# Transformer block with attention and experts on one core: who takes the last head's peaks out of their banks

## The chip, the cores and the metric

The kernel runs on one core of a Trainium2 chip. A core has five engines that run at the same time, each through its own list of instructions, and wait for each other by semaphores: TensorE (matmul), VectorE, ScalarE, GpSimd and SyncE, which starts DMAs. The metric is the time of one execution in microseconds (us), as the median of several runs. Before the change it was 1334.45 us (three runs, 1333.49 to 1334.74).

## The reference, cut to what matters

```python
h = layernorm(x) * (1 + ca) + sa                   # x: 2048 tokens of 128
q, k, v = h @ wq.T, h @ wk.T, h @ wv.T             # 1024 columns each
q, k, v = (a.reshape(1, 16, 2048, 64) for a in (q, k, v))   # 16 heads of 2048 positions of 64
attn = softmax(q @ k^T * 64 ** -0.5) @ v           # for each head: 2048 x 2048 scores
x = x + ga * (attn.reshape(1, 2048, 1024) @ wo.T)
h = layernorm(x) * (1 + cb) + sb
s = sigmoid(h @ gate_w.T); sel = top_k(s + expert_bias, 2)   # 8 experts, 2 for each token
x = x + gb * (shared_expert(h) + sum over the 2 chosen e of
              s_e * w2[e] @ (silu(w1[e] @ (s_e * h)) * (w3[e] @ (s_e * h))))
```

The reshape makes head i out of the tokens 128 i to 128 i + 127: each of them gives 16 of the head's positions. Everything is computed in float32, the scores as three products of a high and a low part.

## The kernel before, in words

**Units.** A head is worked through as two units of half the queries (1024) each, so there are 32 units; the last head is units 30 and 31. A unit goes over 16 tiles of 128 keys. For each tile TensorE makes the scores of 128 keys and 1024 queries in two banks (lines 1230 to 1236, and 1242 for the first two tiles), ScalarE takes their exponential into one of eight buffers `probs` (line 818), TensorE multiplies it by V (line 1254, "a weighing"), and GpSimd adds the tiles up for the softmax's denominator (lines 889 to 903). The scores of tile kt wait for exponential kt - 2.

**Peaks.** Before the exponentials of a unit the kernel needs a shift for each query, from the peak of its scores. These are found a unit ahead, from 16 "pairs" per unit: TensorE multiplies 128 queries by two times 512 keys into banks 6 and 7 (line 1177), and something takes the maximum out of them. There is one such pair of banks in the units, so each pair waits on the semaphore `peak_free` until the pair before is out. Pairs 0 and all even ones, and 15, are taken by VectorE itself, by a maximum straight from the banks (`pair`, line 975). Pairs 1, 3, ..., 13 (`TAKEN`) are first copied by ScalarE into the buffer `peak_copy` (`take_pair`, line 760), which frees the banks, and VectorE takes the maximum of the copy later (`taken`, line 985), which frees `peak_copy` for the next copy (`copy_read`). After pair 15 the maxima go to TensorE to be turned (line 1185), and by DMA to where the next unit's first scores read them.

**The plan.** `side_jobs` writes the order out by hand: a unit has 32 places, four for each two tiles of keys: scores, scores, weighing, weighing. Jobs are put behind a place, and every engine goes through the same list and does its part of each job. Pairs 4 to 15 of the next unit are behind places 1, 3, ..., 23 of a unit, pairs 0 to 3 of the one after that behind places 25 to 31. The maximum of a copied pair ("taken") is two places behind its pair. In unit 30 there are only pairs 4 to 15 (for unit 31), in unit 31 there are none.

**Other jobs of unit 30.** The softmax sum of unit 29 (place 6, line 1267), its inverse in four parts on VectorE (`inv`, places 6, 7, 8 and 10, line 1001), the scaling of the outputs (place 11, line 1008), the output projection (place 22, line 1280). New in the last head is the norm before the experts, for the first 12 blocks of 128 tokens: statistics of four blocks at a time on VectorE behind the pairs at places 5, 9 and 13 (lines 340 and 349), the root on ScalarE behind place 15 (line 368, with a table load for Sqrt and one back to Exp), the reciprocal on VectorE behind place 17 (lines 356, 518, 519), and the norm itself on ScalarE, four blocks each behind places 18, 22 and 26 (line 498).

**Unit 31 and after.** The logits (line 1204, place 4), the gate on VectorE, a chain of ten instructions of which each waits for the one before, but for the pair of comparisons (lines 527 to 543), the token weights turned (line 1209, place 19) and spread by DMA. Then 36 experts' items of 512 tokens: two matmuls (lines 464 and 465), Silu on ScalarE (506), products on VectorE (571, 573), output product (450) for the item before. The tokens of a routed item are weighed ahead of it by line 438: the first three on VectorE, the others on GpSimd, behind its last add (line 889).

Of the kernel before, what the change touches and what calls it, by code (L numbers as in the profile page):

```python
# [35 lines left out]
EARLY_PAIRS = 4  # L36

TAKEN = list(range(1, PEAK_PAIRS - 1, 2))
# [42 lines left out]
def side_jobs(half, sums=True, project=True, pairs=True, early=True, last_head=False):  # L81

    places = [[] for _ in range(4 * PAIRS)]
    for place, (kind, i) in LONG_JOBS[half].items():
        if sums if kind in ("sum", "out") else pairs if kind == "shift" else project:
            places[place].append((kind, i))
    if pairs:
        for i in range(EARLY_PAIRS, PEAK_PAIRS):
            places[2 * (i - EARLY_PAIRS) + 1].append(("pair", i))
    if early:  # L90
        for i in range(EARLY_PAIRS):
            places[2 * (PEAK_PAIRS - EARLY_PAIRS + i) + 1].append(("pair", i))

    for i in TAKEN:
        place = 2 * ((i - EARLY_PAIRS) % PEAK_PAIRS) + 1
        if pairs if i >= EARLY_PAIRS else early:
            places[min(place + 2, 4 * PAIRS - 1)].append(("taken", i))
    if project:
        for place, job in LOW_PLACES[half].items():
            places[place].append(job)  # L100
    if sums:
        for place, job in SCALE_PLACES[half].items():
            places[place].append(job)
    if last_head:
        for place, jobs in LAST_HEAD_PLACES[half].items():
            places[place] += jobs
    return [places[4 * step:4 * step + 4] for step in range(PAIRS)]


def build(nc, x, wq, wk, wv, wo, gate_w, w1, w2, w3, sw1, sw2, sw3, expert_bias, cond, wmod, out):  # L110
    with ExitStack() as ctx:
# [141 lines left out]
        def adds(kt):  # L253


            return kt // 2 + 1 if kt < 4 else kt - 1
# [6 lines left out]
        def units(t):  # L263

            first, last = (isinstance(t, int) and t == 0), (isinstance(t, int) and t == HEADS // 2 - 1)
            for p in (0, 1):
                for half in (0, 1):
                    final_head = last and p == 1
                    plan = side_jobs(half, sums=not (first and p == 0 and half == 0), project=not final_head,
                                     pairs=not (final_head and half == 1), early=not final_head,  # L270
                                     last_head=final_head)
                    yield p, half, t * 2 + p, t * 4 + (2 * p + half), plan
# [15 lines left out]
        END_T = HEADS // 2 - 1  # L288
# [406 lines left out]
        def _(act):  # L695
# [104 lines left out]
            def body(t):  # L800
                local = 0
                for p, half, head, unit, plan in units(t):
                    first = isinstance(t, int) and t == 0 and p == 0 and half == 0
                    last_head = isinstance(t, int) and t == END_T and p == 1
                    if half == 0 and not last_head:
                        copy_head(head + 1)
                    for step, places in enumerate(plan):
                        for place, jobs in enumerate(places):
                            if place < 2:
                                kt = 2 * step + place  # L810
                                act.wait_ge(scored, unit * TILES + (kt + 1))
                                if not (first and kt < PROBS):

                                    old = kt - PROBS
                                    if kt % 2 == 0:
                                        act.wait_ge(pv_done, unit * PAIRS + (old // 2 + 1))
                                    act.wait_ge(added, unit * ADDS + (adds(old % TILES) - (ADDS if old < 0 else 0)))
                                act.activation(probs[:, kt % PROBS, :],  # L818
                                               ps[:, 2 * place:2 * place + 2, :].rearrange("p a b -> p (a b)"),
                                               ACT.Exp, scale=SCALE).then_inc(exped, 1)  # L820

                            for kind, i in sorted(jobs, key=lambda job: job[0] != "pair"):
                                if kind in COUNTED:
                                    side(Job(jobs_at(t) + local), kind, i, 1 - p)
                                if kind == "step k":
                                    round_step(Job(jobs_at(t) + (local - 1)), i, 1 - p, head * 2 + (3 + i))
                                if kind == "pair" and i in TAKEN:
                                    target = unit + (1 if i >= EARLY_PAIRS else 2)
                                    take_pair(i, target * PEAK_PAIRS + i, target)
                                if kind == "sum":  # L830
                                    sums.append(jobs_at(t) + local + 1)
                                if kind in ("turn", "logits", "weights"):
                                    gating_act(act, kind, i)
                                if kind == "root":
                                    layernorm_root(act, range(READY_BLOCKS), 5)
                                if kind == "norm":
                                    norm_act(act, range(4 * i, 4 * i + 4), 2)
                                local += kind in COUNTED
                        if step == 0 and not first:
                            copy_pv(unit, sums[-1] if sums else None)  # L840
# [76 lines left out]
        def _(dve):  # L917
# [121 lines left out]
            def body(t):  # L1039
                local = 0  # L1040
                for p, half, head, unit, plan in units(t):
                    for places in plan:
                        for jobs in places:
                            for kind, i in jobs:
                                job = Job(jobs_at(t) + local)
                                if kind == "pair" and i not in TAKEN:
                                    target = unit + (1 if i >= EARLY_PAIRS else 2)
                                    pair(i, target * PEAK_PAIRS + i, target, PEAK_BANK)
                                if kind == "taken":
                                    target = unit + (1 if i >= EARLY_PAIRS else 2)  # L1050
                                    taken(i, target * PEAK_PAIRS + i, copies(target, i))
                                if kind == "low q":
                                    low_q(Job(jobs_at(t) + (local - 1)), i, 1 - p,
                                          head * CASTS + (CASTS + PROJECTIONS.index(("q", i)) + 1))
                                if kind == "step k":
                                    step_k(Job(jobs_at(t) + (local - 1)), i, head * 2 + (3 + i))
                                if kind == "low k":
                                    low_k(Job(jobs_at(t) + (local - 1)), i, 1 - p, head * 2 + (3 + i))
                                if kind == "inv":
                                    invert(i, Job(jobs_at(t) + (local - 1)))  # L1060
                                if kind == "scale":
                                    scale_outputs(Job(jobs_at(t) + (local - 1)), unit, 1 - half)
                                if kind == "out":
                                    add_head(head - 1, job)
                                if kind == "shift":
                                    keep_shift(job, unit + 1, 1 - half)
                                if kind == "stats":
                                    dve.wait_ge(mid_ready, 4 * i + 4)
                                    layernorm_stats(dve, link, x_mid, range(4 * i, 4 * i + 4))
                                if kind == "rstd":  # L1070
                                    shifts_of(dve, link, range(READY_BLOCKS), 3)
                                if kind == "gate":
                                    dve.wait_ge(consts, 5 + EXPERTS - 1)
                                    gate(dve, link, 0)
                                local += kind in COUNTED
# [305 lines left out]
```

## Time and profile before

| | |
|---|---|
| median of three runs | 1334.45 us |
| time of the profiled execution | 1334.12 us |
| its span, first to last instruction | 1332.3 us |
| TensorE busy | 1307.2 us (98%) |
| VectorE busy | 899.1 us (67%), 1024 instructions |
| ScalarE busy | 864.7 us (65%), 1052 instructions |
| GpSimd busy | 1175.7 us (88%) |
| copies `peak_copy` on ScalarE (line 760) | 215, mean 1016 ns |
| maxima from the banks on VectorE (line 975) | 297, mean 1223 ns |
| maxima from the copy on VectorE (line 985) | 215, mean 1212 ns |

Times in the rows are microseconds from the start of the span. PE is TensorE, PEld its weight loads, DVE VectorE, ACT ScalarE, POOL GpSimd. A busy share is an average over stages; what a stage waits for is read from its own rows. Matmuls overlap: a row of two that lasts 0.50 us may be followed by the next after 0.34.

### The profile page before, as it was taken

Reading aid. Unit: us, or ns where it says so; the run is one execution under the profiler, and the core shown is the slowest. Engines: PE = TensorE matmul, PEld = TensorE weight load, DVE = VectorE, ACT = ScalarE, POOL = GpSimd, SP = SyncE. Lnnn points to the kernel's source line nnn. Section 1 sums busy time; section 2 is a strip of 40 time slices with the busy share of each in tenths; the row PEclk is TensorE's granted clock in tenths of the full one; section 3 lists DMA queues with packets and bytes.
Section 4 is the critical chain, followed back from the end, with each engine's and each line's share of the span. In section 5 each row is a group of like instructions: output and inputs, shape, how many; then the busy total and the mean of one; then the engine's idle time right before and its main releaser. Section 6 shows DMA issues by size and latency. Waiting matters only on the chain.

```text
span 1332.3 us, 21996 instructions
## 1 busy us (share of the span) xinstructions
PE 1307.2 (98%) x8714; PEld 692.3 (52%) x8714; DVE 899.1 (67%) x1024; ACT 864.7 (65%) x1052; POOL 1175.7 (88%) x537
## 2 busy tenths in 40 slices
PE   6999999999999999999999999999999999999998
PEld 5554555454555545454545555554545455454565
DVE  5767667676767676676767676766767676736754
ACT  6676767666766666676767666666767676675331
POOL 2399999999999999999999999999999999989343
PEclk8999999999999999999999999999999999999999
DMA  8020202020100102020201002020202011003222
GB/s 208 3 47 1 49 1 49 1 48 1 36 14 5 45 1 49 1 49 1 48 1 28 21 1 48 2 48 1 49 1 48 1 25 25 1 1 64 71 96 56
DMA packets 31960, 41.53 MB, mean 31 GB/s; under 512 B 4298, under 2 KB 15186, under 8 KB 31858
## 3 DMA queue, kind: packets, MB, share of 16 engines
q1 hardware_dynamic: 31714, 40.13, 12.4%
q8 instruction: 69, 1.13, 0.4%
q14 instruction: 33, 0.27, 0.1%
q10 hardware_dynamic: 144, 0.00, 0.0%
HBM read 13.70 MB, written 1.11 MB: 11 GB/s over the span
## 4 chain that ended last, share of the span: by engine, by line
PE 94%; DVE 3%; ACT 1%; issue 1%; DMA 0%; SPq 0%; ACTq 0%; DVEq 0%
PE ps L1254 35%; PE ps L1177 13%; PE ps L1230 9%; PE ps L1236 9%; PE ps L1233 9%; PE ps L1154 4%; PE ps L1280 2%; PE ps L1158 2%; PE ps L464 2%; PE ps L450 2%; PE ps L1267 2%; PE ps L465 2%; DVE peak_parts L975 1%; PE ps L1242 1%; DMA probs<-in_L_attn_wq_dram 0%
## 5 line engine op out<-in xcount | busy, mean ns | idle before, releaser
L818 ACT ACTIVATE probs<-ps 128x1024 f32<-128x1024 f32 x512 | 498.8, 1033 | 76.8 <-PE ps L1236 72.7
L975 DVE TENSOR_REDUCE peak_parts<-ps 128x2 f32<-128x1024 f32 x297 | 362.2, 1223 | 243.9 <-PE ps L1177 242.3
L1254 PE MATMUL ps<-probs,v_sb 128*64 128x512 f32 x2048 | 522.6, 606 | 0.0
L903 POOL TENSOR_TENSOR acc<-acc,probs 128x1024 f32<-128x1024 f32 x192 | 458.2, 2387 | 31.8 <-ACT probs L818 30.2
L903 POOL TENSOR_TENSOR acc_odd<-acc_odd,probs 128x1024 f32<-128x1024 f32 x192 | 459.7, 2394 | 0.0
L760 ACT COPY peak_copy<-ps 128x1024 f32<-128x1024 f32 x215 | 218.4, 1016 | 247.7 <-PE ps L1177 169.9
L985 DVE TENSOR_REDUCE peak_parts<-peak_copy 128x2 f32<-128x1024 f32 x215 | 260.6, 1212 | 34.1 <-ACT peak_copy L760 34.1
L1254 PEld LDWEIGHTS ps<-probs,v_sb 128*64 128x64 f32 x2048 | 123.8, 136 | 156.6 <-issue 116.0
L1230 PE MATMUL ps<-q_hi,d_hi 64*128 64x512 f32 x512 | 201.6, 394 | 1.2 <-ACT probs L818 1.2
L1230 PE MATMUL ps<-q_hi,d_swap_hi 64*128 64x512 f32 x512 | 201.6, 394 | 0.0
L1236 PE MATMUL ps<-q_hi,d_lo 64*128 64x512 f32 x512 | 200.4, 391 | 0.0
L1236 PE MATMUL ps<-q_hi,d_swap_lo 64*128 64x512 f32 x512 | 200.4, 391 | 0.0
L1233 PE MATMUL ps<-q_lo,d_hi 64*128 64x512 f32 x512 | 199.7, 390 | 0.0
L1233 PE MATMUL ps<-q_lo,d_swap_hi 64*128 64x512 f32 x512 | 199.4, 389 | 0.0
L1177 PE MATMUL ps<-k_hi,q_hi 64*128 64x512 f32 x512 | 120.3, 466 | 4.4 <-DVE d_lo L966 2.3
L1177 PE MATMUL ps<-k_swap_hi,q_hi 64*128 64x512 f32 x512 | 117.8, 456 | 3.5 <-ACT peak_copy L760 1.8
L1177 PEld LDWEIGHTS ps<-k_hi,q_hi 64*128 64x128 f32 x512 | 47.8, 183 | 130.6 <-DVE peak_parts L975 68.1
L1177 PEld LDWEIGHTS ps<-k_swap_hi,q_hi 64*128 64x128 f32 x512 | 48.0, 184 | 127.6 <-DVE peak_parts L975 54.9
L1001 DVE RECIPROCAL ps<-ps 128x128 f32<-128x128 f32 x128 | 112.9, 928 | 0.0
L1233 PEld LDWEIGHTS ps<-q_lo,d_hi 64*128 64x128 f32 x512 | 94.7, 185 | 12.7
L1230 PEld LDWEIGHTS ps<-q_hi,d_swap_hi 64*128 64x128 f32 x512 | 95.0, 186 | 10.5 <-ACT probs L818 0.4
L1236 PEld LDWEIGHTS ps<-q_hi,d_lo 64*128 64x128 f32 x512 | 94.5, 185 | 11.4
(159 smaller groups left out, 1496.9 us busy)
## 6 DMA issues: line engine op xcount, KB each, us to landing
k_swap_hi<-k_hi SPq DMA_DIRECT2D x64, 128.0 KB, 2.3
d_swap_hi<-d_hi SPq DMA_DIRECT2D x64, 128.0 KB, 2.3
d_swap_lo<-d_lo SPq DMA_DIRECT2D x64, 128.0 KB, 2.4
q_hi<-weights_dram SPq DMA_DIRECT2D x8, 256.0 KB, 3.1
q_lo<-weights_dram SPq DMA_DIRECT2D x8, 256.0 KB, 3.2
k_hi<-weights_dram SPq DMA_DIRECT2D x8, 256.0 KB, 3.2
k_swap_hi<-weights_dram SPq DMA_DIRECT2D x8, 256.0 KB, 3.2
probs<-in_L_ffn_w_dram SPq DMA_DIRECT2D x2, 512.0 KB, 5.6
```

The source lines that it names most:

```text
L760: act.copy(peak_copy[:, :, :], ps[:, PEAK_BANK:PEAK_BANK + 2, :]).then_inc(peak_free, 1)
L818: act.activation(probs[:, kt % PROBS, :], ps[:, 2 * place:2 * place + 2, :].rearrange("p a b -> p (a b)"), ACT.Exp, scale=SCALE).then_inc( ...
L903: pool.tensor_tensor(total, total, probs[:, kt % PROBS, :], ALU.add).then_inc(added, 1)
L975: dve.tensor_reduce(peak_parts[:, :, i // STRETCHES, i % STRETCHES], ps[:, bank:bank + 2, :], AX.X, ALU.max).then_inc(peak_free, 1)
L985: dve.tensor_reduce(peak_parts[:, :, i // STRETCHES, i % STRETCHES], peak_copy[:, :, :], AX.X, ALU.max).then_inc(copy_read, 1)
L1001: dve.reciprocal(job.ps[:, cols], job.ps[:, cols]).then_inc(part_inverted, 1)
L1154: mm = pe.matmul(job.ps[at:at + HEAD_DIM, k * P:(k + 1) * P], w[:, col:col + HEAD_DIM], h_head[:, :], start=True, stop=True, tile_position ...
L1177: mm = pe.matmul(ps[:, bank + b, :], q_hi[at, target_parity, q:q + P], keys[at, target_parity, cols], start=True, stop=True, tile_position ...
L1230: pe.matmul(ps[:, slot + b, :], hi[b][at[b], p, cols], q_hi[at[b], p, q], start=kt < 2, stop=False, tile_position=(b * HEAD_DIM, 0), skip_ ...
L1233: pe.matmul(ps[:, slot + b, :], hi[b][at[b], p, cols], q_lo[at[b], p, q], start=False, stop=False, tile_position=(b * HEAD_DIM, 0), skip_g ...
L1236: mm = pe.matmul(ps[:, slot + b, :], lo[b][at[b], p, cols], q_hi[at[b], p, q], start=False, stop=kt >= 2, tile_position=(b * HEAD_DIM, 0), ...
L1254: mm = pe.matmul(ps[at:at + HEAD_DIM, PV_BANK, :], v_sb[:, p, chunk_of(kt) * HEAD_DIM:(chunk_of(kt) + 1) * HEAD_DIM], probs[:, kt % PROBS, ...
```

## The change

In the last head, and only there, no pair is copied. `side_jobs` plans no "taken" job there, ScalarE skips its copies, and VectorE takes the maximum of the odd pairs straight from the banks, at the pair's own place.

```diff
@@ side_jobs
     for i in TAKEN:
         place = 2 * ((i - EARLY_PAIRS) % PEAK_PAIRS) + 1
-        if pairs if i >= EARLY_PAIRS else early:
+        if (pairs if i >= EARLY_PAIRS else early) and not last_head:
             places[min(place + 2, 4 * PAIRS - 1)].append(("taken", i))
@@ ScalarE's body
-                                if kind == "pair" and i in TAKEN:
+                                if kind == "pair" and i in TAKEN and not last_head:
                                     target = unit + (1 if i >= EARLY_PAIRS else 2)
                                     take_pair(i, target * PEAK_PAIRS + i, target)
@@ VectorE's body
                 for p, half, head, unit, plan in units(t):
+
+                    last_head = isinstance(t, int) and t == END_T and p == 1
                     for places in plan:
                         for jobs in places:
                             for kind, i in jobs:
                                 job = Job(jobs_at(t) + local)
-                                if kind == "pair" and i not in TAKEN:
+                                if kind == "pair" and (last_head or i not in TAKEN):
                                     target = unit + (1 if i >= EARLY_PAIRS else 2)
                                     pair(i, target * PEAK_PAIRS + i, target, PEAK_BANK)
```

## Rows read from the trace of the kernel before

**Rows 1.** Busy time by stretches: stretch, its length, each engine's busy time (instructions), clock, DMA.

```profile
1156.60:1180.00 23.40, 19.42 (x134) 9.79 (x134) 16.90 (x40) 17.33 (x23) 19.97 (x10) 1.00 0.00 1
1180.00:1195.00 15.00, 15.00 (x102) 8.85 (x98) 1.67 (x3) 9.35 (x13) 14.61 (x7) 1.00 0.01 1
```

**Rows 2.** Timeline, TensorE, unit 30: start, length, line, tiles, form, [idle before <-releaser]. P7, P10, P12 to P14.

```profile
1156.63 0.51 PE L1177 MATMUL ps<-k_swap_hi,q_hi 64*128 64x512 f32 x2
...
1163.09 0.49 PE L1177 MATMUL ps<-k_swap_hi,q_hi 64*128 64x512 f32 x2 [0.34 <-ACT peak_copy L760]
...
1168.11 0.50 PE L1177 MATMUL ps<-k_hi,q_hi 64*128 64x512 f32 x2 [0.34 <-ACT peak_copy L760]
...
1170.41 0.50 PE L1177 MATMUL ps<-k_hi,q_hi 64*128 64x512 f32 x2
...
1175.40 0.49 PE L1177 MATMUL ps<-k_swap_hi,q_hi 64*128 64x512 f32 x2 [1.45 <-ACT peak_copy L760]
```

**Rows 3.** Timeline, ScalarE, unit 30.

```profile
1168.07 1.28 ACT L368 ACT_TABLE_LOAD   x1
...
1170.99 1.94 ACT L818 ACTIVATE probs<-ps 128x1024 f32<-128x1024 f32 x2
...
1174.35 0.99 ACT L760 COPY peak_copy<-ps 128x1024 f32<-128x1024 f32 x1
```

**Rows 4.** Timeline, VectorE, unit 30.

```profile
1157.18 2.56 DVE L1001 RECIPROCAL ps<-ps 128x128 f32<-128x128 f32 x3
1159.65 1.16 DVE L975 TENSOR_REDUCE peak_parts<-ps 128x2 f32<-128x1024 f32 x1
...
1161.85 0.86 DVE L340 BATCH_NORM_STATS2 stats<-x_mid 128x6 f32<-128x128 f32 x4
...
1163.04 0.93 DVE L1001 RECIPROCAL ps<-ps 128x128 f32<-128x128 f32 x1
1164.00 0.69 DVE L1008 TENSOR_TENSOR oT<-o_raw,ps 128x512 f32<-128x512 f32 x1
1164.61 1.22 DVE L975 TENSOR_REDUCE peak_parts<-ps 128x2 f32<-128x1024 f32 x1
...
1175.94 1.23 DVE L975 TENSOR_REDUCE peak_parts<-ps 128x2 f32<-128x1024 f32 x1 [4.38 <-PE ps L1177]
```

**Rows 5.** Timeline, GpSimd, units 30 and 31, with its last add.

```profile
1181.78 2.37 POOL L903 TENSOR_TENSOR acc<-acc,probs 128x1024 f32<-128x1024 f32 x1 [0.32 <-ACT probs L818]
...
1198.10 3.07 POOL L897 TENSOR_TENSOR acc_odd<-probs 128x1024 f32<-128x1024 f32 x1 [2.19 <-ACT probs L818]
...
1231.48 2.34 POOL L889 TENSOR_TENSOR acc<-acc,acc_odd 128x1024 f32<-128x1024 f32 x1
```

**Rows 6.** Timeline, VectorE and TensorE, the first routed experts.

```profile
1231.62 2.75 DVE L573 TENSOR_TENSOR probs<-probs,q_hi 128x512 f32<-128x512 f32 x1
1231.83 1.02 PE L465 MATMUL ps<-acc,w3T 128*128 128x512 f32 x2
...
1236.10 1.13 PE L464 MATMUL ps<-acc,w1T 128*128 128x512 f32 x2 [0.51 <-DVE acc L438]
...
1240.88 1.02 PE L465 MATMUL ps<-acc,w3T 128*128 128x512 f32 x2
...
1242.63 1.02 PE L464 MATMUL ps<-acc,w1T 128*128 128x512 f32 x2
```

**Rows 7.** Timeline, ScalarE and VectorE, the first root of the prologue.

```profile
3.24 1.28 ACT L368 ACT_TABLE_LOAD   x1
...
4.04 0.18 DVE L349 BATCH_NORM_AGGREGATE mean_var<-stats 128x2 f32<-128x6 f32 x1
```

**Rows 8.** Timeline, VectorE, the gate in unit 31.

```profile
1195.54 0.44 DVE L527 TENSOR_SCALAR wvT<-wvT 128x96 f32<-128x96 f32 x1 [12.69 <-ACT wvT L486]
...
1197.97 0.95 DVE L535 TENSOR_TENSOR wkT<-wvT 128x768 f32<-128x768 f32 x1
...
1207.39 2.35 DVE L543 TENSOR_TENSOR wvT<-wvT 128x96 f32<-128x96 f32 x1
```

## The prediction

> **What bounds the kernel now.** The page's first part (the table above) has TensorE busy for 98% of the span, so the first question is where the last head is not TensorE. The table by stretches answers it [rows 1]: between 1156.6 and 1180.0 us, inside the last head's first unit, TensorE is busy for 19.42 of 23.40 us, and in the next 15 us for all 15.00. So 4.0 us of idle time are there to be had, and nothing in the next stage. I name a pair by its number i and write P10 for TensorE's two matmuls of pair 10; only one pair fits in the two peak banks, so each P waits until the pair before is out. The timeline of TensorE gives the starts [rows 2]: P10 waited 0.34 us and P14 1.45 us, both for ScalarE's copy. ScalarE's timeline shows why P14 is so late [rows 3]: Sqrt's table from 1168.07, the root, Exp's table, two exponentials from 1170.99, four norms (by the code), and only at 1174.35 the copy of pair 13, though P13 had started at 1170.41. VectorE's timeline [rows 4] is a full queue (three inversions, a pair, its copied neighbour, statistics, an inversion, the scaling); what is in front of a pair there is what will hold the bank after the change.
>
> The end hangs on GpSimd as well. Its adds [rows 5] run nearly without a break, with 0.32 us idle before 1181.78 and 2.19 before 1198.10, both for ScalarE's exponentials. Their last one ends at 1231.48 + 2.34 = 1233.82; VectorE's product at 1231.62 lasts 2.75 us, to 1234.37, just behind it, and the third routed expert's matmul starts at 1236.10 [rows 6]. A gain has to pass both engines.
>
> **What goes and what comes.** Units 30 and 31 are the last head, and pairs 4 to 15 of unit 31 are made in unit 30; the four early ones come from the unit before and are unchanged. So five copies (pairs 5, 7, 9, 11, 13; the last one took 0.99 us) go from ScalarE, and five reductions of the copy from VectorE. Five reductions from the banks, of 1.22 or 1.23 us, take their place, earlier in VectorE's order: pair 9 after inversion 3 and before the scaling, pair 11 after the third statistics, pair 13 after the reciprocal of the root. No DMA moves. VectorE's total hardly changes; which pair waits for what changes.
>
> Unit costs, from rows 2 and 4: a pair's start to its reduction 0.54 (1175.40 to 1175.94); reduction 1.22 or 1.23, the next instruction 0.08 before its end (1164.00 + 0.69 against 1164.61), so 1.14 apart; end of a reader to the next P 0.05 (1174.35 + 0.99 to 1175.40); from a P that waited, over two weighings, to the next 2.30 (1168.11 to 1170.41); an inversion 0.82 (a third of 1157.18 to 1159.65); statistics with moments 1.19 (1161.85 to 1163.04).
>
> P5 and P6 move by under 0.15 us, and the sum job behind them waits for GpSimd's last add anyway, so I let P7 stand at 1156.63. Then VectorE: pair 7 from 1157.17; inversions 1 and 2 from 1158.31; pair 8 at 1159.95; statistics at 1161.09; inversion 3 at 1162.28; pair 9 from 1163.10 to 1164.33. P10 is at 1164.38, not 1163.09: **1.29 us lost**, since statistics and an inversion that lay behind a copied pair now lie in front of a bank.
>
> P11 follows at 1166.68. The third statistics start at 1166.06 and end 1.27 later, at 1167.33; pair 11 runs from 1167.25 to 1168.48; P12 at 1168.53 (0.42 late), P13 at 1170.83, pair 13 from 1171.37 to 1172.60, **P14 at 1172.65 instead of 1175.40: 2.75 us gained**, because neither tables nor norms stand in front of the reader any more. On ScalarE the copy of pair 11 no longer precedes the Sqrt load. That load doesn't wait for its operand: in the prologue it starts at 3.24 while the moments end at 4.22 [rows 7]. So the root starts 0.05 after 1167.33 and exponential 8 another 1.62 later (from 1168.07 to 1170.99 are 2.92, less the first load and its gap of 0.02), at 1169.00 instead of 1170.99: 1.99 earlier, in time for P13's followers.
>
> The Trainium skill ("ScalarE: Activation LUTs", What ACT_TABLE_LOAD costs) adds a drain of about 1.38 us to a load of 1.28. The trace has no room for it [rows 3]: two loads, the root and all gaps lie within the 2.92 us from 1168.07 to 1170.99. By the page exponential 8 would be at about 1170.4, P14 at 1173.05, and the gain 2.35: it stands beside rival B.
>
> **What the later stages leave of it.** TensorE is full from 1180 to 1195 [rows 1], so it carries 2.75 on. GpSimd carries less: its backlog moves by the 1.99 of exponential 8 and eats the 0.32 of idle time, 2.34 in all (with 0.03 of overlap). The add before the idle time of 2.19 ended at 1198.10 - 2.19 = 1195.91, and would end at 1193.57. Now the gate [rows 8]. Its first step, at 1195.54, lasts 0.44 us, to the end of that add; it would be issued at 1192.79, and end at 1193.63, thus 2.35 earlier. The comparison of line 535 then comes at 1195.63, but GpSimd's next add, tied to exponentials that moved 2.75, at 1195.35. Before, the add came 0.13 us behind the comparison and lasted 3.07 against 2.37; now it comes in front. I take it that it has the first turn, as soon as line 534 is through (0.09 behind 535's issue, 1195.72), and ends 2.25 later, as 1198.10 + 3.07 = 1201.17 is 2.25 after line 535's end: at 1197.97. Line 535 and the next add then cost one round more, about the 3.07 that a hindered add took, to 1201.04. The rest of the gate, which took 8.57 from 1201.17 to 1207.39 + 2.35 = 1209.74, ends at 1209.61: only 0.13 earlier. TensorE's weight turns wait there, some 2.6 us, and nearly all its lead is gone at the start of the experts. GpSimd loses 0.25 net: three hindered adds as before, and 0.25 on the first (1195.35 to 1197.97 are 2.62, against 2.37). Its last add ends 2.50 earlier, at 1231.32. But there the time comes back: VectorE's product of 1231.62, now at 1231.49, finds GpSimd done and no longer waits for it. TensorE's own queue then sets the third routed expert [rows 6]. From the line 465 matmul before it, over one output product, to its line 464 matmul went 4.27 us (1231.83 to 1236.10); two experts later, unhindered, the same step took 1.75 (1240.88 to 1242.63). So it starts at 1231.83 + 1.75 - 0.13 = 1233.45 instead of 1236.10. **Gain 2.65.** If the comparison keeps its turn instead, gate and GpSimd both move 2.34, and the gain is 2.34. I take 2.6.
>
> That the two block each other for a whole instruction is what the skill states ("SBUF — State Buffer", Who interferes with whom), for two inputs in SBUF against GpSimd's reads, and never for a reduction. The trace agrees: 3.07 against 2.37 us. It says nothing of who is next in line, where my two sums part.
>
> The profiled execution took 1334.12 us around a span of 1332.3; less 2.6 it is 1331.5. The three runs have their median 0.33 higher, at 1334.45: forecast 1331.8.
>
> **Bounds.** The reduction of an odd pair behind VectorE's queue is in no row. Its price at P10 lies between 0 (pair 9 as soon as it is there) and 1.29 plus one statistics, 2.5; the gain at P14 doesn't rest on it if P11 to P13 keep to 2.30, and falls to about 1.5 at the far end. The gate's phase lies between 2.34 earlier and two GpSimd adds later than mine.
>
> **Rivals.** (A) The gate loses one turn more to GpSimd, for example because line 534 is caught too: it ends 2.3 later, at 1211.9, the experts start 2.2 late, the regain of 2.52 leaves 0.3: 1334.1. For it: line 543, on 128x96 elements, lasted 2.35 us, a whole add [rows 8]. Against: only line 535 changes its place by my sum. 10%. (B) Behind an exponential a table load takes twice its row: exponential 8 then starts 1.28 later than by my sum, at 1170.28, P13's followers wait for it and the next one, and P14 is at about 1173.0: 2.4 gained, 1332.1. For it: no load in rows 3 stands behind an exponential. Against: the second one, behind the root, took no more than 1.28 and a gap. 5%. (C) The other side: two turns more than mine, gate at 1214.2; the experts start 4.5 late and regain 2.52: 2.0 lost, 1336.5. It decides from a gate that ends after 1212.3. For it: every wait is a whole add of 2.3. Against: it takes an add 0.6 us earlier than I have it. 8%. (D) VectorE's queue costs more than I have and P14 gains only about 1.5: 1332.9. 12%.
>
> **Numbers.** The forecast has 65%; its own range, 2.2 to 3.2 us gained, is 1331.2 to 1332.3. What a measurement can tell from no change is about 0.2%, here 2.67 us, or 1331.8: the forecast sits on that line, so I give 42 of its 65 to faster and 23 to same, where A, B and D (27) fall too; C is slower. Faster 0.42, same 0.50, slower 0.08. The range goes to A's end and allows 0.3 us for the runs' spread: 1330.9 to 1334.2.
>
> **What would show it.** Right: P10 near 1164.4 after a wait of about 1.4 us for VectorE; ScalarE's Sqrt load right behind exponential 7, well before the root; P14 near 1172.6; the logits 2.7 earlier; line 535 some 3 us long; a wait of 2 to 3 us before the weight turns of line 1209; no long wait of VectorE at line 573. Wrong: P14 not before 1174, a load that waits for the moments, a gate that ends after 1210, or experts whose third product isn't over 2 us earlier.

## The result and the profile after

The changed kernel is slower: 1337.51 us (median of 17 runs, 1335.0 to 1338.34) against 1334.74 us for the kernel before (17 runs, 1333.49 to 1337.21), a ratio of 1.0015 with a 95% interval of [1.0008, 1.0021]. The forecast of 1331.8 us missed it, and so did its range, which ended at 1334.2. The profiled execution took 1337.32 us around a span of 1335.4, against 1334.12 around 1332.3. Lines from 1040 on have moved by two: the pairs are now at line 1179, the weighings at 1256, the output projection at 1282, the weight turns at 1211.

The changed kernel's page, engines and the three peak groups. The change did what it says: five copies fewer, five maxima more from the banks, five fewer from the copy. VectorE is busy for 3.8 us more, which no count explains.

```profile
PE 1310.5 (98%) x8714; PEld 694.9 (52%) x8714; DVE 902.9 (68%) x1024; ACT 860.3 (64%) x1047; POOL 1174.2 (88%) x537
...
L975 DVE TENSOR_REDUCE peak_parts<-ps 128x2 f32<-128x1024 f32 x302 | 368.2, 1222 | 239.6 <-PE ps L1179 237.9
...
L760 ACT COPY peak_copy<-ps 128x1024 f32<-128x1024 f32 x210 | 213.2, 1015 | 240.6 <-PE ps L1179 166.8
L985 DVE TENSOR_REDUCE peak_parts<-peak_copy 128x2 f32<-128x1024 f32 x210 | 254.5, 1212 | 34.1 <-ACT peak_copy L760 34.1
```

Its TensorE timeline in unit 30: P10, P12, P13, P14, the weighing and the output projection behind it, P15.

```profile
1164.44 0.50 PE L1179 MATMUL ps<-k_swap_hi,q_hi 64*128 64x512 f32 x2 [1.21 <-DVE peak_parts L975]
...
1168.56 0.50 PE L1179 MATMUL ps<-k_hi,q_hi 64*128 64x512 f32 x2
...
1170.86 0.51 PE L1179 MATMUL ps<-k_hi,q_hi 64*128 64x512 f32 x2
...
1176.03 0.50 PE L1179 MATMUL ps<-k_swap_hi,q_hi 64*128 64x512 f32 x2 [3.27 <-DVE peak_parts L975]
1176.46 1.55 PE L1256 MATMUL ps<-probs,v_sb 128*64 128x512 f32 x4
1177.79 3.16 PE L1282 MATMUL ps<-wo,oT 128*64 128x128 f32 x32
...
1181.75 0.50 PE L1179 MATMUL ps<-k_swap_hi,q_hi 64*128 64x512 f32 x2
```

P10 to P13 are where the forecast had them [rows 2]. P14 is not: it comes at 1176.03, 0.63 us later than before, where 2.75 earlier was forecast. VectorE's timeline of the same stretch shows what held pair 13:

```profile
1169.11 1.23 DVE L975 TENSOR_REDUCE peak_parts<-ps 128x2 f32<-128x1024 f32 x1 [0.60 <-PE ps L1179]
1170.25 0.22 DVE L356 RECIPROCAL rstd<-std 128x12 f32<-128x12 f32 x1
1170.50 2.06 DVE L518 TENSOR_TENSOR shift_ln<-mean_var,rstd 128x12 f32<-128x12 f32 x1
1172.59 2.26 DVE L519 TENSOR_SCALAR shift_ln<-shift_ln 128x12 f32<-128x12 f32 x1
1174.77 1.21 DVE L975 TENSOR_REDUCE peak_parts<-ps 128x2 f32<-128x1024 f32 x1
```

Two instructions on 128x12 elements take 4.3 us. Before, the same two took 0.17 us each, at 1171.17 and 1171.38, as VectorE's timeline of the kernel before has them:

```profile
1170.92 0.22 DVE L356 RECIPROCAL rstd<-std 128x12 f32<-128x12 f32 x1
1171.17 0.17 DVE L518 TENSOR_TENSOR shift_ln<-mean_var,rstd 128x12 f32<-128x12 f32 x1
1171.38 0.17 DVE L519 TENSOR_SCALAR shift_ln<-shift_ln 128x12 f32<-128x12 f32 x1
```

GpSimd's timeline of the changed kernel has the other side. Line 518 ends with the first of these adds (1170.15 + 2.38 = 1172.53), line 519 with the second (1172.48 + 2.34 = 1174.82):

```profile
1170.15 2.38 POOL L903 TENSOR_TENSOR acc<-acc,probs 128x1024 f32<-128x1024 f32 x1 [1.44 <-ACT probs L818]
1172.48 2.34 POOL L903 TENSOR_TENSOR acc_odd<-acc_odd,probs 128x1024 f32<-128x1024 f32 x1
```

and GpSimd's timeline of the kernel before shows why they didn't meet there: the add came when both were done, after a long idle time.

```profile
1172.09 2.38 POOL L903 TENSOR_TENSOR acc<-acc,probs 128x1024 f32<-128x1024 f32 x1 [3.35 <-ACT probs L818]
```

The add waits for exponential 8, and ScalarE's timeline of the changed kernel has that one at 1169.05, 1.94 earlier than before [rows 3]. The norms wait for line 519 too:

```profile
1164.53 1.28 ACT L368 ACT_TABLE_LOAD   x1
1167.43 0.30 ACT L368 ACTIVATE std<-mean_var,eps 128x12 f32<-128x12 f32 x1 [1.62 <-DVE mean_var L349]
...
1169.05 1.94 ACT L818 ACTIVATE probs<-ps 128x1024 f32<-128x1024 f32 x2
1174.89 1.65 ACT L498 ACTIVATE x_in<-x_mid,shift_ln,rstd 128x128 f32<-128x128 f32 x4 [3.90 <-DVE shift_ln L519]
```

The second loss is TensorE's clock. By the table of stretches the granted clock is still at 0.96 in the first stretch behind the wait of 3.27 us, which ended at 1176.03, and at 0.50 (1.2 of 2.4 GHz) in the three us after that:

```profile
1176.00:1177.00 1.00, 0.97 (x6) 0.44 (x8) 0.43 (x1) 1.00 (x3) 0.00 (x0) 0.96 0.00 0
1177.00:1180.00 3.00, 3.00 (x26) 2.39 (x24) 0.80 (x1) 2.89 (x6) 2.48 (x2) 0.50 0.03 5
1180.00:1181.00 1.00, 1.00 (x16) 0.93 (x14) 0.00 (x0) 0.00 (x0) 1.00 (x1) 0.83 0.00 0
```

The output projection takes 3.16 us instead of 1.92 and the weighing 1.55 instead of 1.08: 1.71 together. So P15 is 2.31 later (1181.75 against 1179.44), and the logits as much (1194.61 against 1192.31). Behind the logits the clock falls once more (0.50 from 1198 to 1200). The third routed expert is 2.61 later (1238.71, against 1236.10 in [rows 6]). TensorE waits for VectorE there, whose product of line 573 is again held by GpSimd's last add, and that add comes at 1234.08 instead of 1231.48. The three timelines, TensorE, VectorE and GpSimd:

```profile
1238.71 1.13 PE L464 MATMUL ps<-acc,w1T 128*128 128x512 f32 x2 [0.52 <-DVE acc L438]
...
1235.36 1.62 DVE L573 TENSOR_TENSOR probs<-probs,q_hi 128x512 f32<-128x512 f32 x1
...
1234.08 2.35 POOL L889 TENSOR_TENSOR acc<-acc,acc_odd 128x1024 f32<-128x1024 f32 x1
```

The rest of the 3.1 us of span is one meeting of VectorE and GpSimd more, of 0.47, near 1285, where a product of line 573 takes 1.81 us; a second profile of the kernel before has it too.

The gate never met the order that I feared, since the whole stage comes 2.3 later. VectorE's timeline of the changed kernel, gate:

```profile
1197.84 0.45 DVE L527 TENSOR_SCALAR wvT<-wvT 128x96 f32<-128x96 f32 x1 [12.67 <-ACT wvT L486]
...
1200.28 0.95 DVE L535 TENSOR_TENSOR wkT<-wvT 128x768 f32<-128x768 f32 x1
1201.27 0.96 DVE L537 TENSOR_TENSOR wkT<-wkT,earlier 128x768 f32<-128x768 f32 x1
1202.26 3.03 DVE L539 TENSOR_TENSOR wqT<-wqT,wkT 128x768 f32<-128x768 f32 x1
...
1207.62 2.34 DVE L543 TENSOR_TENSOR wvT<-wvT 128x96 f32<-128x96 f32 x1
```

### The profile page after: what moved, and what is told of

It reads as the page before. It is cut to its first block, busy times and chain, and to the rows that moved or that the text cites. A ratio compares the mean times of both kernels' runs of the same rounds, so it can differ in the third digit from the quotient of the medians.

```text
span 1335.4 us, 21986 instructions
## 1 busy us (share of the span) xinstructions
PE 1310.5 (98%) x8714; PEld 694.9 (52%) x8714; DVE 902.9 (68%) x1024; ACT 860.3 (64%) x1047; POOL 1174.2 (88%) x537
## 4 chain that ended last, share of the span: by engine, by line
PE 94%; DVE 4%; ACT 1%; DMA 0%; issue 0%; SPq 0%; DVEq 0%; ACTq 0%
PE ps L1256 36%; PE ps L1179 13%; PE ps L1232 9%; PE ps L1238 9%; PE ps L1235 9%; PE ps L1156 4%; PE ps L1282 2%; PE ps L1160 2%; PE ps L1269 2%; PE ps L464 2%; PE ps L450 2%; PE ps L465 2%; DVE peak_parts L975 1%; PE ps L1244 1%; DVE ps L1001 0%; DVE probs L573 0%
## 5 line engine op out<-in xcount | busy, mean ns | idle before, releaser
L975 DVE TENSOR_REDUCE peak_parts<-ps 128x2 f32<-128x1024 f32 x302 | 368.2, 1222 | 239.6 <-PE ps L1179 237.9
L760 ACT COPY peak_copy<-ps 128x1024 f32<-128x1024 f32 x210 | 213.2, 1015 | 240.6 <-PE ps L1179 166.8
L985 DVE TENSOR_REDUCE peak_parts<-peak_copy 128x2 f32<-128x1024 f32 x210 | 254.5, 1212 | 34.1 <-ACT peak_copy L760 34.1
```

Source lines behind the costliest of these rows:

```text
L760: act.copy(peak_copy[:, :, :], ps[:, PEAK_BANK:PEAK_BANK + 2, :]).then_inc(peak_free, 1)
L975: dve.tensor_reduce(peak_parts[:, :, i // STRETCHES, i % STRETCHES], ps[:, bank:bank + 2, :], AX.X, ALU.max).then_inc(peak_free, 1)
L985: dve.tensor_reduce(peak_parts[:, :, i // STRETCHES, i % STRETCHES], peak_copy[:, :, :], AX.X, ALU.max).then_inc(copy_read, 1)
```

## The experiments

The theory: lines 518 and 519 need a memory path that a GpSimd add holds for its whole length; the change moves exponential 8, and with it the add, in front of them. The rival: something in VectorE's own queue (the root's late result, the pairs ahead) makes them long. Times stand beside the kernel before, run on the same chip in the same set of runs. The timelines of the experiments lie up to 1.0 us before or behind those of the two kernels above, from the start on, so that a start is compared across kernels only to about that.

**The two instructions off the shared path.** The shift goes through a free piece of a PSUM bank: the reciprocal is written there too, and one instruction with a single input in SBUF makes the shift.

```diff
+            if nth == 3:
...
+                link(dve.reciprocal(bank, std[:, at]))
+                dve.scalar_tensor_tensor(shift_ln[:, at], mean_var[:, at, 0], -1.0, bank,
+                                         ALU.mult, ALU.mult).then_inc(shift_ln_ready, 1)
```

> The changed kernel, but for the first 12 blocks VectorE writes the reciprocal of the root a second time into unused columns of the job bank (PSUM) and makes the norm's shift in one instruction from the mean (SBUF) and that bank, in place of the two instructions of lines 518 and 519. Theory (port): in the changed kernel lines 518 and 519 lasted 2.06 and 2.26 us, not 0.17, because GpSimd's adds hold what they share with a VectorE instruction on SBUF alone, and pair 13 stands behind them. Then here the shift takes 0.2 to 0.3 us, pair 13 starts near 1171.4, P14 near 1172.7 (1176.0 changed, 1175.4 before), TensorE idles under 0.3 us there, its granted clock stays at 1.00, and the kernel takes 2 to 3 us less than before, 5 to 6 less than the changed one. Rival (queue): the direct reductions themselves fill VectorE; then pair 13 starts after 1174 still, P14 after 1175, and the time is within 1 us of the changed kernel's.

Measured: 1332.14 us (11 runs) against 1334.54, ratio 0.9983 [0.9974, 0.9992]. VectorE's timeline, unit 30 and the gate:

```profile
1170.80 0.18 DVE L522 RECIPROCAL ps<-std 128x12 f32<-128x12 f32 x1
1171.02 0.17 DVE L523 SCALAR_TENSOR_TENSOR shift_ln<-mean_var,ps 128x12 f32<-128x12 f32 x1
1171.82 1.23 DVE L985 TENSOR_REDUCE peak_parts<-ps 128x2 f32<-128x1024 f32 x1 [0.64 <-PE ps L1189]
...
1196.12 3.14 DVE L545 TENSOR_TENSOR wkT<-wvT 128x768 f32<-128x768 f32 x1
1199.30 0.96 DVE L547 TENSOR_TENSOR wkT<-wkT,earlier 128x768 f32<-128x768 f32 x1
```

and TensorE's, with P14 and the output projection:

```profile
1173.10 0.49 PE L1189 MATMUL ps<-k_swap_hi,q_hi 64*128 64x512 f32 x2
...
1174.44 1.92 PE L1292 MATMUL ps<-wo,oT 128*64 128x128 f32 x32
```

GpSimd's add of tile 8 runs from 1170.58 as early as in the changed kernel, right beside lines 522 and 523, and they aren't held. P14 comes without a wait, the projection has the full clock (behind the logits it falls here too, to 0.50 from 1194 to 1197), and the second comparison (line 535, here 545) takes 3.14 us behind an add issued at 1196.09, as the prediction had it.

**The add out of the way instead.** VectorE keeps the changed kernel's instructions; GpSimd's add of tile 8 in unit 30 waits until line 519 is through.

```diff
+                    if unit == UNITS - 2 and kt == PROBS:
+                        pool.wait_ge(shift_ln_ready, 2)
```

> The changed kernel, with one wait more on GpSimd and nothing else: in unit 30 its add of tile 8 (the one right behind exponential 8) waits until VectorE's lines 518 and 519 are through. VectorE's instructions and their order are those of the changed kernel. Theory 1 (the two small instructions are held, each for a whole add, by GpSimd at the memory they share): they take 0.17 us each again instead of 2.06 and 2.26, pair 13 starts at about 1171.4 instead of 1174.77 and P14 at about 1172.8 instead of 1176.03, the out projection behind it keeps the full clock (1.92 us, not 3.16), GpSimd's add of tile 8 starts about 1.5 us later than in the changed kernel, at about 1171.7, and the time is 2 to 5 us below the changed kernel's, about the time of the kernel before or up to 2.5 below it (1332 to 1335), depending on what the gate makes of the new phase. Theory 2 (something in VectorE's own queue makes them long, the root's late result or the pairs before them): they stay near 2 us each, P14 stays near 1176, and the time is the changed kernel's, 1337.5.

Measured: 1333.6 us (11 runs) against 1334.51, ratio 0.9996 [0.9987, 1.0005], whose interval lies wholly below the changed kernel's [1.0008, 1.0021]. VectorE's timeline:

```profile
1170.66 0.17 DVE L518 TENSOR_TENSOR shift_ln<-mean_var,rstd 128x12 f32<-128x12 f32 x1
1170.86 0.17 DVE L519 TENSOR_SCALAR shift_ln<-shift_ln 128x12 f32<-128x12 f32 x1
1171.57 1.23 DVE L977 TENSOR_REDUCE peak_parts<-ps 128x2 f32<-128x1024 f32 x1 [0.53 <-PE ps L1181]
...
1196.66 3.13 DVE L535 TENSOR_TENSOR wkT<-wvT 128x768 f32<-128x768 f32 x1
1199.83 3.00 DVE L537 TENSOR_TENSOR wkT<-wkT,earlier 128x768 f32<-128x768 f32 x1
1202.86 3.02 DVE L539 TENSOR_TENSOR wqT<-wqT,wkT 128x768 f32<-128x768 f32 x1
```

and GpSimd's, the add that waited:

```profile
1171.12 2.39 POOL L905 TENSOR_TENSOR acc<-acc,probs 128x1024 f32<-128x1024 f32 x1 [2.25 <-DVE shift_ln L519]
```

The same two instructions, in the same queue, take 0.17 us each; P14 comes at 1172.85 and the clock stays full from 1173 to 1182. From both sides the add is the cause, and the rival falls. In the gate three instructions in a row are held, so it ends at 1210.56, later than before (1209.74), although it began 2.55 earlier.

**Half of the change.** Only pair 13 is taken from the banks; the other odd pairs are copied as before.

```diff
+DIRECT = (13,)
...
-                                if kind == "pair" and i in TAKEN and not last_head:
+                                if kind == "pair" and i in TAKEN and not (last_head and i in DIRECT):
```

> The kernel before with only pair 13 taken straight from its banks in the last head; pairs 5, 7, 9 and 11 are copied as before. Port theory: exponential 8 stays at about 1171.0, so GpSimd is idle until about 1172.1 while lines 518 and 519 run in 0.17 us each from 1171.2; pair 13 runs at about 1171.6 to 1172.8, and P14 is only held by its scores, at 1173.7 to 1173.9: 1.5 to 1.7 us earlier than before; time 1 to 1.7 us below before. Queue theory: a direct pair behind the reciprocal costs what it did in the changed kernel: P14 after 1175, time not below before.

Measured: 1333.75 us (11 runs), ratio 1.0001 [0.9992, 1.001]. Exponential 8 stays at 1171.09, so the add stays behind the two small instructions (0.17 us each), and P14 comes at 1173.89, 1.5 earlier than before. TensorE's timeline shows where that goes, the weight turns behind a gate that ends at 1211.61:

```profile
1211.76 1.03 PE L1215 MATMUL ps<-ident,wvT 128*8 128x128 f32 x8 [1.98 <-DVE wvT L547]
```

So 1.5 us were gained ahead of the gate, and little or nothing of it was left in the end, where 1 to 1.7 were expected. The ratio is one of means, and counts two executions of over 1338 us that the median leaves aside.

**The other part.** The same edit with three early pairs.

```diff
+DIRECT = (5, 7, 9)
```

> The kernel before with pairs 5, 7 and 9 taken straight from the banks in the last head, 11 and 13 copied. Port theory: P10 is 1.3 us late (1164.4) as in the changed kernel, but the copy of pair 11 stands in front of the Sqrt load, exponential 8 is at about 1171.3 or later, GpSimd is idle while lines 518 and 519 run (0.17 us each), P14 is at 1175.5 to 1176.0 behind the copy of pair 13, the clock stays at 1.00: time 0 to 0.6 us above before. Queue theory: three of the five direct reductions bring three fifths of the loss, 1.8 us above before.

Measured: 1334.91 us (11 runs), ratio 1.0003 [0.9995, 1.0012]. P10 comes at 1164.18 after a wait of 1.23 us, as in the changed kernel; exponential 8 stays at 1170.96 and P14 at 1175.38. The 1.1 us lost at P10 cost nothing, because the long waits behind it stay where they were. What moved exponential 8 in the changed kernel is then most likely the copy of pair 11, which stood ahead of the root's table load: it is the only copy that both halves leave in place. That was not tried alone.

**The wait filled.** The changed kernel, and 26 small matmuls more (64x256) ahead of P14, into a free piece of a bank. TensorE works through the wait; P14 is held as before.

```diff
+                if i == 14 and isinstance(target_head, int) and target_head == HEADS - 1 and target_half == 1:
+                    for n in range(FILL):
+                        pe.matmul(ps[:, JOB_BANK, 256:512], q_hi[0:HEAD_DIM, target_parity, 0:P],
+                                  k_hi[0:HEAD_DIM, target_parity, 0:256], start=True, stop=True, tile_position=(0, 0))
```

> The changed kernel with 26 extra matmuls of 256 columns into unused columns of the job bank, in TensorE's queue just before pair 14 (last head's first unit only), where it was idle for 3.27 us; nothing reads them. Theory (clock as a second part of the loss): P14 stays near 1176.0 and VectorE's pair 13 near 1174.8, but the granted clock stays at 1.00 behind it, so that the output projection (line 1282) takes 1.9 us and not 3.2, P15 is near 1180.2 instead of 1181.75, and if the second fall at 1197.3 was of the same making, that goes too: 1.3 to 3.4 us below the changed kernel. Rival: the clock fell for another reason than the idle time: it falls here as well, and the time is the changed kernel's.

Measured: 1335.06 us (11 runs), ratio 1.0005 [0.9996, 1.0014]: 0.5 us above the kernel before where the changed kernel was 2.8 above it, by the medians; the intervals of the two ratios still overlap, from 1.0008 to 1.0014. The span is 1333.0 against 1335.4. TensorE's timeline, whose rows lie 0.9 before the changed kernel's:

```profile
1171.68 3.27 PE L1170 MATMUL ps<-k_hi,q_hi 64*128 64x256 f32 x26
1175.22 0.50 PE L1184 MATMUL ps<-k_swap_hi,q_hi 64*128 64x512 f32 x2 [0.26 <-DVE peak_parts L976]
```

and its table of stretches, with the full clock behind P14:

```profile
1176.00:1182.00 6.00, 6.00 (x58) 3.60 (x55) 2.69 (x4) 4.56 (x8) 5.10 (x3) 1.00 0.00 0
```

Lines 518 and 519 are as long as in the changed kernel (2.07 and 2.33), P14 is as late, and the loss against the kernel before is gone within the error. By the rows, what made the change slower, and not merely useless, was the clock's fall behind the wait. The second fall, behind the logits, was not of that making: it is here as before (0.50 from 1195 to 1198).

**Both kernels once more.** No edit: one more execution and profile of each, for what in them is chance.

> The kernel before, unchanged, for a second profile. In the first one the granted clock stayed at 1.00 behind the logits (1192.3 to 1195.2); in the changed kernel and in the four experiments so far it fell to 0.50 for some 3.3 us there. Theory (a phase that one profile happened to miss): this profile of the kernel before shows that fall too, between 1194 and 1200, and the gate and end stand 1 to 2 us later than in the first. Rival (the change makes the fall): 1.00 throughout from 1150 to 1320, as before.

> The changed kernel, unchanged, for a second profile. Lines 518 and 519 again last over 1.5 us each, TensorE again idles some 3.3 us before P14, and the clock falls to 0.50 behind it: all theories expect that, since it doesn't hang on a phase. The second fall, behind the logits, is there or not by the theory of a phase, and always there by the rival.

Measured: before 1335.05 us, its P14 at 1175.81 and the clock full from 1176 to 1182 and from 1190 to 1204. After 1336.95 us, its P14 at 1176.56 with a wait of 3.31 us and a mean clock of 0.72 from 1176 to 1182, but with the full clock from 1190 to 1204. So the fall behind P14 belongs to the change (both of its profiles). The one behind the logits does not, for the changed kernel can be without it; that the kernel before would show it in this profile was expected and did not come true, though the next experiment has it there without the change.

**The same edit on the kernel before.** The shift in PSUM, copies as before: if it saves time there, the first experiment says nothing of the change.

```diff
+                link(dve.reciprocal(bank, std[:, at]))
+                dve.scalar_tensor_tensor(shift_ln[:, at], mean_var[:, at, 0], -1.0, bank,
+                                         ALU.mult, ALU.mult).then_inc(shift_ln_ready, 1)
```

> The kernel before with the PSUM form of the norm's shift from e1 and nothing else (all odd pairs copied). Control: in the kernel before lines 518 and 519 took 0.17 us each, since GpSimd was idle there, and VectorE then waited 4.38 us for pair 14. Port theory: nothing to gain, time within 0.5 us of before, P14 at 1175.4 as before. Rival (the new form is worth something in itself): 1 us or more faster than before.

Measured: 1335.35 us (11 runs) against 1335.02, ratio 1.0 [0.9991, 1.0008]; P14 waits 1.44 us for ScalarE's copy as ever. Its clock falls behind the logits too (from 1196 to 1199.8), with nothing of the change in it.

**The gate off the shared path.** The shift in PSUM on the changed kernel, and in the first gate one input of each instruction in the peak banks, which are free by then.

```diff
+                dve.tensor_tensor(greater[:, at], other, mine, ALU.is_gt)
+                link(dve.tensor_tensor(eq, other, mine, ALU.is_equal))
+                link(dve.tensor_tensor(eq, eq, earlier[:, None, :, :].broadcast_to(
+                    [P, n, EXPERTS, EXPERTS]), ALU.mult))
```

(`other` and `eq` lie in PSUM, `mine` and `earlier` in SBUF.)

> e1 with the first gate rewritten so that no VectorE instruction has two inputs in SBUF: sigmoid's denominator, score, a second copy of the biased score, the comparison for equality and the rank go to the free peak banks; one addition more. Port theory: the gate's steps fall from 3.0 to about 0.95 us (comparisons) and from 2.37 and 1.28 to under 0.3 (the last two), the gate from 12.4 us from its start to its end, as in e1 (14.2 before), to 6.5 to 7.5; no add of GpSimd beside it lasts over 2.5 us, its last add ends 1.4 to 2 us earlier than in e1 against the logits, and the kernel takes 0.8 to 1.7 us less than e1. Rival (the long steps are these shapes' own cost, or reading PSUM costs as much): gate and time as e1.

Measured: 1330.35 us (6 runs) against 1335.02, ratio 0.9965 [0.9952, 0.9978]: the fastest version here, faster than both kernels. One of the six took 7156.49 us and is not in the ratio; without it the median is 1330.11. VectorE's timeline of its gate, first, middle and last:

```profile
1193.83 0.26 DVE L543 TENSOR_SCALAR ps<-wvT 128x96 f32<-128x96 f32 x1 [12.69 <-ACT wvT L486]
...
1196.26 0.96 DVE L550 TENSOR_TENSOR ps<-ps,wvT 128x768 f32<-128x768 f32 x1
1197.25 0.97 DVE L551 TENSOR_TENSOR ps<-ps,earlier 128x768 f32<-128x768 f32 x1
...
1200.53 0.25 DVE L556 TENSOR_TENSOR wvT<-wvT,ps 128x96 f32<-128x96 f32 x1
```

The gate takes 6.95 us (1193.83 to 1200.78) instead of 14.20 before [rows 8], GpSimd's adds beside it at most 2.40 instead of 3.07 and more, its last add comes at 1227.89, and the third routed expert at 1231.85 without a wait.

**That gate on the kernel before.** The same gate, with nothing of the change.

> The kernel before, with nothing of the change, and the first gate (of 12 blocks) with one input of each two-input instruction in the peak banks instead of in SBUF; the last head's pairs are as before, copied. Theory 1 (GpSimd and VectorE hold each other only where both of VectorE's inputs lie in SBUF): the gate takes about 7 us instead of 14.2, its comparisons 0.95 each, GpSimd's adds beside it 2.37 instead of 3.07, its last add ends 1 to 2 us earlier, the wait of TensorE before the third routed expert (0.51) goes, and the time is 1 to 2.5 us below the kernel before: 1332.5 to 1334. So the 4.7 us of the kernel that had both this and the shift in the banks would be roughly the sum of the two parts, some 2.5 and some 2. Theory 2 (the gate has slack: only the pairs count): the time is within 0.5 us of the kernel before.

Measured: 1331.68 us (11 runs) against 1334.51, ratio 0.9981 [0.9972, 0.999]. The gate takes 6.95 us (1195.80 to 1202.75), and the third routed expert no longer waits. What was expected of GpSimd did not come: its last add starts at 1231.41, against 1231.48. This profile has the clock's fall behind the logits, and at 1333.3 its execution was among the three slowest of the eleven. By the medians the two edits nearly add up: 1.9 parts in a thousand for the gate, 1.7 for the pairs with the shift in PSUM, and 3.5 for both.

## Why the prediction was wrong

**Right.** P10: forecast 1164.38, measured 1164.44; the wait was for VectorE, 1.21 us. Sqrt's load: it didn't wait for its operand and ran at 1164.53, right behind the exponentials. Exponential 8: 1169.00 against 1169.05, and no drain beside the loads. P12 and P13: 1168.53 and 1170.83 against 1168.56 and 1170.86. The bound of the end by GpSimd and the regain at the third routed expert held: with both sources of holds gone (the gate off the shared path) it starts 4.25 earlier and waits for nobody.

**The step that failed** is the one that puts pair 13 "after the reciprocal of the root" and lets it run "from 1171.37". It takes lines 518 and 519 as the 0.17 us each that they were, while the step before it moves exponential 8 by 1.99 us. GpSimd's add hangs on that exponential: before, it started 1.10 behind it (1172.09 against 1170.99), so from 1169.00 it starts at about 1170.1, and by the sum's own steps the two instructions come at about 1170.5. Both numbers follow from the prediction's terms, and I didn't lay them beside each other. I weighed the lock at the gate, 25 us later, because the rows before show it there, and not where the change itself made it new. It cost 4.0 us on VectorE (2.06 + 2.26 less 0.34), so that P14 lost 0.63 instead of gaining 2.75. With the add held back, P14 came at 1172.85, or where the forecast had it within the offset of the timelines. I also told the Trainium skill's rule ("SBUF — State Buffer", Who interferes with whom) too narrowly, as one for two inputs in SBUF. The page adds that `tensor_scalar` can take the shared ports too, in its two-port modes. The runs agree: line 519, with one input, was held for 2.26 us, and line 527, which begins inside an add, took 1.81 us with pair 13 alone, where its form into PSUM took 0.26 inside an add. And the prediction has it wrong that the section says nothing of who is next in line: it says that the order of issue decides who blocks. That is its first sum, and the rows agree: line 535, issued at 1196.12 behind an add of 1196.09, let the add go first.

**The second miss** is the clock, which stood in no term. P14's wait grew from 1.45 to 3.27 us, and behind the longer one the granted clock was 0.50 for three us: 1.71 us more on two groups of matmuls, and with the wait filled a median 0.5 instead of 2.8 us above the kernel before. Both stretches of the kernel before had a clock of 1.00 [rows 1], so they couldn't price it; that a wait twice as long could set it off should have been a bound.

**The bound that was too tight.** The prediction says of the price of an odd pair behind VectorE's queue that "the gain at P14 doesn't rest on it". That was true of what was lost at P10, but pair 13 is itself such a pair. Its price had its far end in the prediction's own rule, a whole add for each instruction held, or 4.7 us; no bound of mine used it there. Rivals A, B and C didn't come about in the changed kernel. D, a gain of 1.5 at P14, named the right place, VectorE's queue, with a price that had no mechanism behind it: 1.25 us, where the step was off by 3.38.

**The gate, had the step held.** The lost turn was real: line 535 took 3.14, 3.14 and 3.13 us in the three versions in which P14 was early, behind an add issued just ahead of it. Its sum came out differently each time: in the first experiment line 537 found a gap and the gate ended at 1208.00, 1.7 before the kernel before's; with the add held back it ended 0.8 later, and with pair 13 alone 1.9 later, close to rival A's 2.2. So the repaired versions gain 2.4, 0.9 and 0.8 us by their medians, against my 2.6, but only the first gain is clear of the noise (ratios 0.9983, 0.9996 and 1.0001). That the gate's end sets their order is not shown: the profiled executions of the first two took 1332.56 and 1332.47 us, with the third routed expert at 1234.42 and 1234.41. Nor is an earlier gate enough: with pairs 5, 7 and 9 it ended at 1207.62, 2.1 before the kernel before's, GpSimd's last add came at 1231.76, no earlier, and the time was the same. Not settled: what the clock's fall behind the logits costs, and how often it comes (in 8 of the 12 profiles, with and without the change). It moves exponentials there and so may decide who meets whom.

## What to carry to other kernels

When a change makes one engine's result earlier, follow who is released by it, and lay the new start beside every small instruction of the engine that shares a path with that one: a hold costs the length of the other's instruction, whatever the size of one's own. Put an operand or the result of VectorE's instructions into PSUM where GpSimd streams through SBUF; that took two holds out of the last head and halved the gate. Price a wait of TensorE not by its length alone where it grows to a few us, but also by what stands behind it if the clock falls.

## What the hardware showed beyond expectation

- 128x12 elements, 0.17 us, took 2.06 and 2.26 us beside adds of 2.38 and 2.34. The reciprocal of the same size in between (line 356, 0.22 us from 1170.25) ran beside the first of these adds unhindered.
- The rows of the gate fit one order: of two instructions that need the path, the one issued first has it to its end. Line 535 at 1197.97 had it before an add at 1198.10 (0.95); at 1196.12 behind one of 1196.09 it took 3.14.
- A wait of TensorE of 3.27 to 3.31 us was followed by half the clock about 1 us later, for some 3.4 us, in both profiles of the changed kernel; waits of 1.44 to 1.46 us at the same place were not.
- The clock also fell behind the logits, 24 matmuls with outputs of 128x8 in a stretch without idle time, in one execution of the changed kernel (0.50 from 1198) and not in another.
